# Partition sums by bf16 matmuls, and new orders of work for all five engines, in a decoder layer of attention, cross attention and quantised feed-forward

## The chip, the cores and the metric

The kernel runs on one core of a Trainium2 chip. A time is the device time of one execution in microseconds (us). Before the change, three executions took 2735.64, 2737.21 and 2741.36 us (median 2737.21). The program runs TensorE (PE in the rows, PEld for its weight loads), VectorE (DVE), ScalarE (ACT), GpSimd (POOL) and SyncE (SP), which here issues all DMAs from one queue.

## The reference

The input is 64 independent sequences of 128 tokens by 512 features, with a context of the same shape.

```python
x = layernorm(x + self_attention(x, Wqkv, q_norm_w, k_norm_w, Wo))   # 16 heads, rmsnorm, rope, causal
x = layernorm(x + cross_attention(x, ctx, ctx))                      # 8 heads over the feature axis
x = layernorm(x + quant_dequant(x) @ quant_dequant(W).T)             # fp8 e4m3 in blocks of 128

def cross_attention(q, k, v):          # per batch: q, k, v are 128 x 512; 8 heads of 16 rows
    qk = einsum('bdm,bdn->bmn', qh, kh) * 16 ** -0.5      # 512 x 512 per head
    return einsum('bmn,bcn->bcm', softmax(qk), vh)
```

The kernel keeps fp32-like accuracy by splitting operands in a high and a low fp16 part, and for that scales the input and the context of each batch by a power of two. That power is taken from the sum of squares over the whole 128 x 512 block: ScalarE squares and sums along each partition (`xss`, `css`, 128 x 1 in fp32), TensorE sums over the 128 partitions, and VectorE takes the exponent. Only the exponent of the sum is used.

## The kernel before, in words

One batch is 128 x 512 and is small; the work of a batch is a long chain through all engines. The kernel therefore runs as a pipeline by hand. Each engine has a table (`SP_STEPS`, `POOL_STEPS`, `ACT_STEPS`, `DVE_STEPS`, `PE_STEPS`) with one entry per step of a batch, written `name:part@stage`. In slot t an engine goes through its table once, and does each step for batch t minus stage. A full slot so holds one batch's worth of every step, from up to nine different batches. The tables alone set each engine's order; the engines are held together only by semaphores, and each does its instructions in order, so that one that waits holds up all behind it. The first slots and the last ones are unrolled with the steps of absent batches left out, the middle is a loop over two slots. Where a table is cut into a slot does not matter, only the order of its entries counting stage by stage: with all entries of a table turned round, the instruction stream stays the same.

What the steps are that this text speaks of, with their lines:

- TensorE: `cross_scores` n = 0 to 15 (L1085, into `mx`, two matmuls of 512 columns side by side), read by VectorE's `cross_max` (L811); `cross_scores_T` n = 0 to 15 (L1099, into `st`), read by ScalarE's exponential `probs` (L645); `cross_pv` (L1112); `proj_q`, `proj_k`, `proj_v` and `ffn` in four parts each (L983, three matmuls a part); `proj_o` (L975); `self_scores` (L1017 and L1020), `self_scores_T` (L1030), `self_pv` (L1048, L1051); `context_T` (L968); `x_sum` (L991, L992) and `ctx_sum` (L1073, L1074), the sums over partitions. `mx` and `st` have one buffer each: the next scores wait until the last are read.
- `x_sum` and `ctx_sum` are each two matmuls with one output column: a 128 x 128 matrix of ones times the 128 sums, and the ones times `tiny` (2 to the power -70), which keeps the sum off zero. In fp32 each shows as two passes in the trace (x2). TensorE also does this once for the weights (L956, L957).
- Feed-forward: VectorE and GpSimd quantise in turns (`quant_scale` L920 to L925, `quant_unit` L581, `quant_magic`, `quant_round` L588, L591, L594), ScalarE and GpSimd split the result (`xd_high` L732, `xd_low` L603), the queue transposes it to `xdT` (`turn_xd` L465), and `ffn` reads that.
- Self attention: `rope_terms` (VectorE, L872), `rope_sum` (GpSimd, L547, L548), `part_high` (ScalarE, L675, L676), `part_low` (GpSimd, L552), the transposes `turn_parts` (L414) to `qs` and `ks`; `self_probs` (ScalarE, L695), `mask` (GpSimd, L558), `self_pv`.
- The queue also loads the next context, `ld_cx` (L368). It overwrites the only buffer `cx`, so it waits until `context_T` of the batch before is done.

Of the kernel before, what the change touches and what calls it, by code (L numbers as in the profile page):

```python
# [5 lines left out]
def post_ln_decoder_kernel(nc, x, ctx_in, wqkv, q_norm_w, k_norm_w, wo, wffn, cos_t, sin_t, out):  # L6
    F32, F32R = mybir.dt.float32, mybir.dt.float32r
    BF16, F16, I32 = mybir.dt.bfloat16, mybir.dt.float16, mybir.dt.int32
# [41 lines left out]
    with es:  # L50
        def sb(name, shape, dt=F32):
            return es.enter_context(nc.sbuf_tensor(name, shape, dt))
# [139 lines left out]
        POOL_STEPS = steps("""
            ctx_scale:0@4 layer_rstd:0@3 layer_mean:2@8 context_low:0@4 layer_rstd:2@8 layer_mean:1@7
            mean_square:0@1 layer_rstd:1@7 rope_sum:0@1 mean_square:1@1 part_low:0@1 quant_unit:0@7
            mask:0@2 mask:1@2 rope_sum:1@1 mask:2@2 mask:3@2 cross_scale:0@6 quant_round:0@7
            query_low:0@3 part_low:1@1 oT_low:0@2 quant_round:1@7 quant_round:2@7 xd_low:0@7
            x_scale:0@0 x_low:0@0 cross_scale:1@6 layer_mean:0@2""")
        ACT_STEPS = steps("""
            probs:8@6 layernorm:0@3 square:0@1 layer_devs:1@7 probs:9@6 layernorm:1@7 probs:10@6
            square:1@1 part_high:0@1 self_probs:0@2 probs:11@6 query_high:0@3 value:0@1  # L200
            self_probs:1@2 probs:12@6 x_square:0@0 self_probs:2@2 probs:13@6 self_probs:3@2
            part_high:1@1 probs:14@6 probs:15@6 oT_high:0@2 probs:0@5 context_out:0@4 probs:1@5
            ctx_square:0@3 xd_high:0@7 probs:2@5 x_high:0@0 probs:3@5 probs:4@5 layer_devs:0@2
            probs:5@5 context_high:0@3 probs:6@5 layer_devs:2@7 probs:7@5 layernorm:2@7""")
        DVE_STEPS = steps("""
            self_shift:0@2 cross_max:12@5 rope_terms:0@1 cross_max:13@5 quant_scale:0@7
            cross_max:14@5 cross_max:15@5 rope_terms:1@1 cross_shift:0@5 cross_max:0@4 cross_turn:0@6
            cross_max:1@4 quant_magic:0@7 cross_max:2@4 self_recip:0@2 self_norm:0@2 cross_max:3@4
            x_exp:0@0 cross_max:4@4 cross_turn:1@6 cross_max:5@4 add_self:0@2 cross_max:6@4
            self_max:0@1 ctx_exp:0@3 self_max:1@1 cross_max:7@4 self_max:2@1 cross_max:8@4  # L210
            ctx_inv:0@4 add_ffn:0@7 cross_max:9@4 self_max:3@1 cross_max:10@4 add_cross:0@6
            cross_max:11@4""")
        PE_STEPS = steps("""
            cross_scores_T:10@6 proj_k:2@1 proj_k:3@1 cross_scores:14@5 proj_v:0@1 proj_v:1@1
            self_scores_T:0@2 cross_scores_T:11@6 cross_scores:15@5 proj_v:2@1 proj_v:3@1
            self_scores_T:1@2 cross_scores_T:12@6 cross_scores:0@4 cross_pv:3@6 self_pv:0@2
            self_scores_T:2@2 cross_scores_T:13@6 self_pv:1@2 cross_scores:1@4 self_scores_T:3@2
            cross_pv:4@6 self_pv:2@2 cross_scores:2@4 cross_scores_T:14@6 self_pv:3@2 cross_pv:5@6
            cross_scores_T:15@6 cross_scores:3@4 cross_pv:6@6 context_T:0@4 cross_scores_T:0@5
            x_sum:0@0 cross_pv:7@6 cross_scores:4@4 cross_scores_T:1@5 proj_o:0@2 proj_o:1@2  # L220
            cross_scores:5@4 cross_scores_T:2@5 proj_o:2@2 proj_o:3@2 cross_scores:6@4
            cross_scores_T:3@5 self_scores:0@1 self_scores:1@1 ctx_sum:0@3 cross_pv:0@5
            cross_scores:7@4 cross_scores_T:4@5 self_scores:2@1 ffn:0@7 ffn:1@7 cross_scores_T:5@5
            cross_scores:8@4 ffn:2@7 ffn:3@7 cross_scores_T:6@5 cross_scores:9@4 proj_q:0@0
            self_scores:3@1 cross_scores_T:7@5 cross_scores:10@4 proj_q:1@0 proj_q:2@0
            cross_scores_T:8@5 cross_scores:11@4 proj_q:3@0 proj_k:0@0 proj_k:1@0 cross_scores:12@4
            cross_scores_T:9@5 cross_pv:1@5 cross_pv:2@5 cross_scores:13@4""")
# [924 lines left out]
```

## Time and profile before

| | |
|---|---|
| three timed executions | 2735.64, 2737.21, 2741.36 us |
| the profiled execution | 2741.84 us, its span 2740.1 us |
| TensorE matmuls | 2488.1 us busy, 91% |
| VectorE | 2203.3 us, 80% |
| ScalarE | 2074.7 us, 76% |
| GpSimd | 1670.0 us, 61% |
| mean granted TensorE clock | 0.971 of full speed |

The busy shares are means over the set-up (about 68 us, until the first `x_sum`), the filling of the pipeline, a long steady state, and the run-out in which ever fewer steps are left in a slot. In the steady state the time is the length of a slot times the number of slots, so it is that stretch that has to be read: which engine never waits in it, and for what it waits when it does. The 1.7 us between the span and the time of the same execution lie outside the span.

### The profile page before, as it was taken

The page shows a single profiled execution, that of the slowest core. Times are in us where ns is not written, and L with a number is a line of the kernel's source. Part 1 is how long each engine was busy: PE and PEld are TensorE (multiplying, and loading weights), DVE is VectorE, ACT ScalarE, POOL GpSimd, SP SyncE. Part 2 cuts the span into 40 slices and gives each one's busy share as a digit, 9 for nine tenths or more (in the row PEclk, how much of TensorE's full clock was granted, in tenths as well). Part 3 has the DMA queues.
Part 4 walks back from the last instruction along what each step waited for, and adds up shares of the span by engine and source line. Part 5 has one row for each costly group of instructions (what it writes and reads, how often), then busy time and mean ns, then how long its engine had stood idle before and what let it go on. Part 6 is the DMA issues. An engine that isn't in the chain of part 4 may idle for free.

```text
span 2740.1 us, 67073 instructions
## 1 busy us (share of the span) xinstructions
PE 2488.1 (91%) x19220; PEld 992.2 (36%) x19220; DVE 2203.3 (80%) x3525; ACT 2074.7 (76%) x3097; POOL 1670.0 (61%) x2586
## 2 busy tenths in 40 slices
PE   0679999999999999999999999999999999998874
PEld 0333333343334333333333333433333333433211
DVE  5258888888888888888888888888888888888651
ACT  2237787788888888888888888888888888887553
POOL 1454666666666666666667666666666666765322
PEclk9889999999999999999999999999999999999876
DMA  2345554544454445444554445544544454544211
GB/s 88 66 103 121 119 125 114 129 123 121 119 129 119 128 112 131 121 128 112 127 128 125 115 119 132 123 118 122 128 119 123 117 131 120 130 115 115 71 41 28
DMA packets 610637, 312.01 MB, mean 114 GB/s; under 512 B 469504, under 2 KB 551424, under 8 KB 610560
## 3 DMA queue, kind: packets, MB, share of 16 engines
q1 hardware_dynamic: 610560, 311.06, 45.1%
q8 instruction: 39, 0.64, 0.1%
q14 instruction: 38, 0.31, 0.0%
HBM read 124.80 MB, written 85.46 MB: 77 GB/s over the span
## 4 chain that ended last, share of the span: by engine, by line
PE 65%; SPq 11%; DMA 9%; issue 5%; DVE 5%; POOL 3%; ACT 2%; ACTq 0%; POOLq 0%; DVEq 0%
PE bank L983 25%; PE pv L1112 13%; PE mx L1085 8%; PE st L1099 7%; DMA xdT<-xd 7%; SPq L414 5%; PE bank L1048 2%; PE bank L1030 2%; PE bank L975 2%; PE bank L1051 2%; DVE nm L811 2%; SPq L388 2%; SPq L398 1%; PE bank L968 1%; SPq L379 1%
## 5 line engine op out<-in xcount | busy, mean ns | idle before, releaser
L811 DVE TENSOR_REDUCE nm<-mx 128x2 f32<-128x1024 f32 x1024 | 1248.5, 1219 | 248.7 <-PE mx L1085 241.9
L645 ACT ACTIVATE pp<-st,esc 128x1024 f32<-128x1024 f32 x1024 | 1139.3, 1113 | 341.8 <-PE st L1099 339.1
L1112 PE MATMUL pv<-pp,vT 128*32 128x512 f32 x4096 | 550.3, 622 | 1.2 <-DVE o2t L906 0.9
L983 PE MATMUL bank<-w_h,xsT 128*128 128x512 f16 x1536 | 525.0, 384 | 9.3 <-DMA xsT<-xs 6.3
L1085 PE MATMUL mx<-kp,qp 48*128 48x512 f16 x2048 | 400.7, 388 | 36.9 <-DVE nm L811 34.4
L1099 PE MATMUL st<-qp,kp 50*128 50x512 f16 x2048 | 401.2, 388 | 25.0 <-ACT pp L645 25.0
L983 PE MATMUL bank<-w_l,xsT 128*128 128x512 f16 x768 | 293.0, 381 | 0.0
L983 PE MATMUL bank<-wf_h,xdT 128*128 128x512 f16 x512 | 180.2, 394 | 83.2 <-DMA xdT<-xd 83.1
L983 PEld LDWEIGHTS bank<-w_h,xsT 128*128 128x128 f16 x1536 | 150.1, 98 | 278.2 <-issue 131.1
L534 POOL TENSOR_SCALAR neg_mean<-total 128x1 f32<-128x1 f32 x192 | 36.5, 190 | 329.3 <-DVE yout L938 207.2
L558 POOL TENSOR_SCALAR_AFFINE_SELECT p<-p 128x512 f32<-128x512 f32 x256 | 168.3, 657 | 108.1 <-ACT p L695 103.1
L1085 PEld LDWEIGHTS mx<-kp,qp 48*128 48x128 f16 x2048 | 99.4, 94 | 354.9 <-DVE nm L811 229.4
L872 DVE SCALAR_TENSOR_TENSOR rope<-bank,rms,rope_w 128x1024 f32<-128x1024 f32 x128 | 163.4, 1277 | 37.6 <-POOL rms L514 19.9
L841 DVE TENSOR_REDUCE nm<-bank 128x4 f32<-128x512 f32 x256 | 174.6, 683 | 14.9 <-PE bank L1020 14.9
L1099 PEld LDWEIGHTS st<-qp,kp 50*128 50x128 f16 x2048 | 99.5, 94 | 219.4 <-ACT pp L645 120.9
L695 ACT ACTIVATE p<-bank 128x512 f32<-128x512 f32 x256 | 156.1, 610 | 24.2 <-PE bank L1030 24.1
L511 POOL TENSOR_SCALAR rms<-ssq,xeps 128x1 f32<-128x1 f32 x128 | 33.9, 265 | 192.6 <-ACT junk L669 192.4
L552 POOL TENSOR_TENSOR qkn<-rope,qkn 128x512 f16<-128x512 f32 x128 | 148.0, 1156 | 3.2 <-ACT qkn L676 3.2
L1112 PEld LDWEIGHTS pv<-pp,vT 128*32 128x32 f32 x4096 | 93.6, 110 | 141.4 <-issue 131.8
L711 ACT ACTIVATE x<-x,shift,rstd 128x512 f32<-128x512 f32 x128 | 103.3, 807 | 48.5 <-POOL shift L543 48.5
L975 PE MATMUL bank<-wo_h,oT_h 128*128 128x512 f32 x256 | 116.7, 456 | 6.6 <-POOL oT_l L574 6.6
L539 POOL TENSOR_SCALAR rstd<-devs 128x1 f32<-128x1 f32 x192 | 36.6, 190 | 133.6 <-ACT junkd L706 123.2
(166 smaller groups left out, 4614.1 us busy)
## 6 DMA issues: line engine op xcount, KB each, us to landing
qp<-q_rows SPq DMA_DIRECT2D x256, 96.0 KB, 2.3
kp<-k_rows SPq DMA_DIRECT2D x256, 96.0 KB, 2.2
xb<-x SPq DMA_DIRECT2D x64, 256.0 KB, 2.8
xr<-x SPq DMA_DIRECT2D x64, 256.0 KB, 2.7
x_rows<-x SPq DMA_DIRECT2D x64, 256.0 KB, 2.1
cx<-ctx SPq DMA_DIRECT2D x64, 256.0 KB, 3.0
...
```

Source lines behind the costliest of these rows:

```text
L552: g_.tensor_tensor(qkn[k][:, :, 2 - k, :], rope[:, 0].rearrange("p h a d -> p h (a d)"), qkn[k][:, :, 0, :], ALU.subtract).then_inc(s_part ...
L558: g_.affine_select(out=p1[c % 2][:], in_=p1[c % 2][:], compare_op=ALU.is_ge, fill=0.0, base=0, pattern=[[0, HC], [1, P]], channel_multipli ...
L645: a.activation(pp[:, unit % PB, 2 * l:2 * (l + 1), :], st[:], ACT.Exp, scale=esc[b.i][:])\
L695: a.activation(p1[c % 2][:], at(f"s1t{c}")[:].rearrange("p (h q) -> p h q", h=HC), ACT.Exp, scale=SELF_SCALE).then_inc(bank_free[BANK[f"s1 ...
L811: v.tensor_reduce(cols, mx[:], AX.X, ALU.max, negate=True).then_inc(mx_free, 1)
L841: v.tensor_reduce(nm1[:, HC * c:HC * (c + 1)], at(f"s1m{c}")[:].rearrange("p (h k) -> p h k", h=HC), AX.X, ALU.max, negate=True).then_inc( ...
L872: v.scalar_tensor_tensor(rope[:].rearrange("p t h a d -> p t (h a d)"), at("qk"[k])[:].unsqueeze(1).to_broadcast([P, 2, D]), rms[:, k:k + ...
L975: last = t.matmul(at(name)[:], a[:, rows], w[:, part, cols], start=(part == 0 and i == 0), stop=(part == KC - 1 and i == 2))
L983: last = t.matmul(at(name)[:], lin[:, KC * lo + part, :], w[:, part, cols], start=(part == 0 and i == 0), stop=(part == KC - 1 and i == 2))
L1085: last = t.matmul(mx[:, q, :], qp[b.i][rows, p, c * P:(c + 1) * P], kp[b.i][rows, p, :], start=True, stop=True)
L1099: last = t.matmul(st[:, q, :], kp[b.i][rows, p, i * P:(i + 1) * P], qp[b.i][rows, p, :], start=True, stop=True)
L1112: last = t.matmul(pv[32 * j:32 * j + 2 * XD, :], vT[b.i][:, i, GROUPS * j + g, :], pp[:, unit % PB, j, :], start=(i == 0), stop=(i == KC - 1))
```

## The change

Two edits. First, the ones and `tiny` become bf16, and the moving operand of the sums becomes the upper half of each fp32 word, read in place as bf16 (the lower 16 bits are cut off). `tiny` is two columns wide instead of one. Second, all five tables are written anew. The latest stage goes from 8 to 9, and so there is one slot more (73 for 72); that comes from where the tables are cut, and most steps keep their place relative to the other steps of their engine.

```diff
-        css, cbits, ones = sb("css", [P, 1]), sb("cbits", [P, 1], I32), sb("ones", [P, P])
-        xss, xbits, tiny = sb("xss", [P, 1]), sb("xbits", [P, 1], I32), sb("tiny", [P, 1])
+        css, cbits, ones = sb("css", [P, 1]), sb("cbits", [P, 1], I32), sb("ones", [P, P], BF16)
+        xss, xbits, tiny = sb("xss", [P, 1]), sb("xbits", [P, 1], I32), sb("tiny", [P, 2], BF16)
...
         SP_STEPS = steps("""
-            ld_kp:1@5 st_qpl:0@4 ld_qp:1@5 turn_xd:0@8 turn_x:0@1 ld_x2r:0@7 ld_qp:0@4 ld_x:0@0
...
+            st_sh1:0@3 st_kpl:0@5 st_out:0@9 ld_sh1:0@3 ld_kp:0@5 st_sh2:0@6 ld_sh2:0@6
...
-            t.matmul(mx[:, 0, 0:2], ones[:], wsum[:], start=True, stop=False)
-            t.matmul(mx[:, 0, 0:2], ones[:], tiny[:].to_broadcast([P, 2]), start=False, stop=True).then_inc(u_wtot, 1)
+            t.matmul(mx[:, 0, 0:2], ones[:], wsum[:].bitcast(BF16).rearrange("p (n a) -> p n a", a=2)[:, :, 1], start=True, stop=False)
+            t.matmul(mx[:, 0, 0:2], ones[:], tiny[:], start=False, stop=True).then_inc(u_wtot, 1)
...
-                t.matmul(at("xt")[:, 0:1], ones[:], xss[:], start=True, stop=False)
-                t.matmul(at("xt")[:, 0:1], ones[:], tiny[:], start=False, stop=True).then_inc(bank_full[BANK["xt"]], 1)
+                t.matmul(at("xt")[:, 0:1], ones[:], xss[:].bitcast(BF16)[:, 1:2], start=True, stop=False)
+                t.matmul(at("xt")[:, 0:1], ones[:], tiny[:, 0:1], start=False, stop=True).then_inc(bank_full[BANK["xt"]], 1)
...
-                t.matmul(at("ct")[:, 0:1], ones[:], css[:], start=True, stop=False)
-                t.matmul(at("ct")[:, 0:1], ones[:], tiny[:], start=False, stop=True).then_inc(bank_full[BANK["ct"]], 1)
+                t.matmul(at("ct")[:, 0:1], ones[:], css[:].bitcast(BF16)[:, 1:2], start=True, stop=False)
+                t.matmul(at("ct")[:, 0:1], ones[:], tiny[:, 0:1], start=False, stop=True).then_inc(bank_full[BANK["ct"]], 1)
```

The queue (SP), from the transpose of the query parts to that of the scaled input. `qs` and `ks` are the transposed self-attention parts, `cx` the context, `kp` and `qp` the cross-attention operands, `q_rows` their copy in memory. Before:

```order
L414 DMA_TRANSPOSE qs<-qkn 128x16x128
L368 DMA cx<-ctx 128x512
L414 DMA_TRANSPOSE ks<-qkn 128x16x128
L388 DMA kp<-k_rows 48x2x512 x2
L379 DMA q_rows<-qpl 128x2x512
L380 DMA q_rows<-qpl 128x512
L398 DMA qp<-q_rows 48x2x512 x2
L465 DMA_TRANSPOSE xdT<-xd 128x8x128
L407 DMA_TRANSPOSE xsT<-xs 128x8x128
L458 DMA x<-x_rows 128x512
```

After:

```order
L414 DMA_TRANSPOSE qs<-qkn 128x16x128
L450 DMA x_rows<-x 128x512
L414 DMA_TRANSPOSE ks<-qkn 128x16x128
L388 DMA kp<-k_rows 48x2x512 x2
L368 DMA cx<-ctx 128x512
L465 DMA_TRANSPOSE xdT<-xd 128x8x128
L398 DMA qp<-q_rows 48x2x512 x2
L379 DMA q_rows<-qpl 128x2x512
L380 DMA q_rows<-qpl 128x512
L407 DMA_TRANSPOSE xsT<-xs 128x8x128
L361 DMA xr<-x 128x512
```

The transpose to `xdT` now comes right behind the load of `cx`, ahead of the load of `qp` and the two stores of `q_rows`; the load of `cx` moved behind the transpose to `ks` and the load of `kp`; the store of `x_rows` moved in, and the load of `xr` comes half a slot earlier.

GpSimd (POOL), from the low part of the queries (`qkn`, L552) through the masks (L558) to the low part of the attention output (`oT_l`). Before:

```order
L552 TENSOR_TENSOR qkn<-rope,qkn 128x16x32
L581 TENSOR_TENSOR yq<-x,qri 128x512
L558 AFFINE_SELECT p_0<-p_0 128x512
L558 AFFINE_SELECT p_1<-p_1 128x512
L547 TENSOR_TENSOR rope<-rope 128x16x16
L548 TENSOR_TENSOR rope<-rope 128x16x16
L558 AFFINE_SELECT p_0<-p_0 128x512
L558 AFFINE_SELECT p_1<-p_1 128x512
L609 TENSOR_TENSOR o2n<-o2t,r 128x16x16
L588 TENSOR_TENSOR yq<-yq,yc 128x512
L599 TENSOR_TENSOR qpl<-x,qpl 128x512
L552 TENSOR_TENSOR qkn<-rope,qkn 128x16x32
```

After:

```order
L558 AFFINE_SELECT p_0<-p_0 128x512
L552 TENSOR_TENSOR qkn<-rope,qkn 128x16x32
L558 AFFINE_SELECT p_1<-p_1 128x512
L581 TENSOR_TENSOR yq<-x,qri 128x512
L547 TENSOR_TENSOR rope<-rope 128x16x16
L548 TENSOR_TENSOR rope<-rope 128x16x16
L558 AFFINE_SELECT p_0<-p_0 128x512
L558 AFFINE_SELECT p_1<-p_1 128x512
L588 TENSOR_TENSOR yq<-yq,yc 128x512
L552 TENSOR_TENSOR qkn<-rope,qkn 128x16x32
L591 TENSOR_TENSOR yq<-yq,yc 128x512
L574 TENSOR_TENSOR oT_l<-o,oT_h 128x512
```

The two masks of the first half come before `quant_unit` (L581), the low part of the queries between them. The low part of the cross-attention query (`qpl`) and one scaling (`o2n`) left this stretch; they come behind the low part of `xd` (L603) now.

TensorE, the four `self_pv` (L1048, L1051) and what lies between them. Before:

```order
L1112 MATMUL pv<-pp,vT 32x512 x4
L1048 MATMUL bank<-p_0,va 32x128 x4
L1051 MATMUL bank<-p_0,sums_of 32x128 x4
L1030 MATMUL bank<-qs,ks 128x128 x4
L1099 MATMUL st<-qp,kp 128x512 x2
L1048 MATMUL bank<-p_1,va 32x128 x4
L1051 MATMUL bank<-p_1,sums_of 32x128 x4
L1085 MATMUL mx<-kp,qp 128x512 x2
L1030 MATMUL bank<-qs,ks 128x128 x4
L1112 MATMUL pv<-pp,vT 32x512 x4
L1048 MATMUL bank<-p_0,va 32x128 x4
L1051 MATMUL bank<-p_0,sums_of 32x128 x4
```

After:

```order
L1051 MATMUL bank<-p_0,sums_of 32x128 x4
L1030 MATMUL bank<-qs,ks 128x128 x4
L1048 MATMUL bank<-p_1,va 32x128 x4
L1051 MATMUL bank<-p_1,sums_of 32x128 x4
L1099 MATMUL st<-qp,kp 128x512 x2
L1030 MATMUL bank<-qs,ks 128x128 x4
L1085 MATMUL mx<-kp,qp 128x512 x2
L1112 MATMUL pv<-pp,vT 32x512 x4
L1048 MATMUL bank<-p_0,va 32x128 x4
L1051 MATMUL bank<-p_0,sums_of 32x128 x4
L1048 MATMUL bank<-p_1,va 32x128 x4
L1051 MATMUL bank<-p_1,sums_of 32x128 x4
```

Parts 0 and 1 come sooner behind one another, and parts 2 and 3 (the last four rows) have nothing between them; before, a `cross_scores` and a `cross_scores_T` stood there. On the whole table, `cross_scores_T` moved forward by three to eight places against the other steps of TensorE, `context_T` back by six, and `ffn:0` forward by one.

On ScalarE, `part_high:0` moved from ahead of `self_probs:0` to behind `probs:12` (before: `square:1 part_high:0 self_probs:0 probs:11`; now: `probs:11 square:1 self_probs:0 probs:12 part_high:0`).

## Rows read from the trace of the kernel before

**Rows 1.** Windows of two stretches: length; PE, PEld, DVE, ACT, POOL busy; clock, DMA share
```profile
600.00:2200.00 1600.00, 1557.19 (x12351) 626.91 (x12348) 1389.73 (x2227) 1319.89 (x1978) 1068.91 (x1647) 1.00 0.49 123
2470.00:2741.00 271.00, 190.48 (x1116) 53.60 (x1112) 148.05 (x230) 151.58 (x194) 96.57 (x155) 0.78 0.24 61
```

**Rows 2.** All waits of TensorE's matmuls from 600 to 2200 us (total, times, longest)
```profile
PE bank L983 <- DMA xdT<-xd: 41.4, 41, 1.5
```

**Rows 3.** Timeline of TensorE (start, duration, ...), the first and last full slot's sum
```profile
249.44 0.38 PE L991 MATMUL bank<-xss,ones 128*128 128x1 f32 x2
...
2466.09 0.38 PE L991 MATMUL bank<-xss,ones 128*128 128x1 f32 x2
```

**Rows 4.** Timeline of TensorE, the two sums and what follows each
```profile
1379.59 0.38 PE L991 MATMUL bank<-xss,ones 128*128 128x1 f32 x2
...
1380.12 1.07 PE L1112 MATMUL pv<-pp,vT 128*32 128x512 f32 x8
...
1386.83 0.33 PE L1073 MATMUL bank<-css,ones 128*128 128x1 f32 x2
...
1387.31 1.06 PE L1112 MATMUL pv<-pp,vT 128*32 128x512 f32 x8
```

**Rows 5.** Weight loads of TensorE by line: bf16, and fp32 of one sum
```profile
L1017 PEld LDWEIGHTS bank<-maskb,identb 128*128 128x128 bf16 x256 | 24.9, 97 | 71.1 <-issue 61.3 <-DVE nm L841 1.8 <-DVE cbits L827 0.9
L992 PEld LDWEIGHTS bank<-tiny,ones 128*128 128x128 f32 x128 | 19.9, 196 | 0.0
```

**Rows 6.** Timeline of TensorE, starts from which the prices are read, and the feed-forward product
```profile
1353.57 0.39 PE L983 MATMUL bank<-wf_h,xdT 128*128 128x512 f16 x1
...
1354.97 0.39 PE L1099 MATMUL st<-qp,kp 50*128 50x512 f16 x2
...
1355.51 0.39 PE L983 MATMUL bank<-w_h,xsT 128*128 128x512 f16 x1
...
1370.43 1.06 PE L1112 MATMUL pv<-pp,vT 128*32 128x512 f32 x8
1371.31 0.40 PE L1048 MATMUL bank<-p,va 128*32 128x128 f32 x8
...
1371.87 0.40 PE L1030 MATMUL bank<-qs,ks 98*128 98x128 f16 x4
1372.19 0.39 PE L1099 MATMUL st<-qp,kp 50*128 50x512 f16 x2
...
1375.71 0.42 PE L1048 MATMUL bank<-p,va 128*32 128x128 f32 x8
...
1390.20 0.39 PE L983 MATMUL bank<-wf_h,xdT 128*128 128x512 f16 x1 [0.73 <-DMA xdT<-xd]
```

**Rows 7.** Timeline of the DMA queue's issues (SP)
```profile
1379.51 0.48 SPq L368 DMA_DIRECT2D cx<-ctx  x1
...
1386.90 1.25 SPq L465 DMA_TRANSPOSE xdT<-xd  x1
```

**Rows 8.** DMA issues from 600 to 2200 us, median us to landing
```profile
xdT<-xd SPq DMA_TRANSPOSE x41, 3.2
```

**Rows 9.** Timeline of GpSimd, same slot
```profile
1367.82 1.16 POOL L552 TENSOR_TENSOR qkn<-rope,qkn 128x512 f16<-128x512 f32 x1
1368.94 1.04 POOL L581 TENSOR_TENSOR yq<-x,qri 128x512 f32<-128x512 f32 x1
...
1372.55 0.73 POOL L548 TENSOR_TENSOR rope<-rope 128x256 f32<-128x256 f32 x1
...
1374.85 0.72 POOL L558 TENSOR_SCALAR_AFFINE_SELECT p<-p 128x512 f32<-128x512 f32 x1 [0.85 <-ACT p L695]
...
1384.30 1.17 POOL L603 TENSOR_TENSOR xd<-yq,xd 128x512 f16<-128x512 f32 x1 [0.80 <-ACT xd L732]
```

**Rows 10.** Timeline of ScalarE, same slot
```profile
1367.07 0.62 ACT L676 ACTIVATE qkn<-rope 128x512 f16<-128x512 f32 x1
...
1368.40 1.11 ACT L645 ACTIVATE pp<-st,esc 128x1024 f32<-128x1024 f32 x1
```

More of the change, by code:

```diff
@@ L188, in post_ln_decoder_kernel @@
         SP_STEPS = steps("""
-            ld_kp:1@5 st_qpl:0@4 ld_qp:1@5 turn_xd:0@8 turn_x:0@1 ld_x2r:0@7 ld_qp:0@4 ld_x:0@0
-            st_out:0@8 st_sh1:0@2 st_kpl:0@4 ld_sh1:0@2 ld_kp:0@4 st_sh2:0@5 st_x2:0@3 ld_xr:0@2
-            ld_sh2:0@5 turn_parts:0@1 ld_cx:0@3 turn_parts:1@1""")
+            st_sh1:0@3 st_kpl:0@5 st_out:0@9 ld_sh1:0@3 ld_kp:0@5 st_sh2:0@6 ld_sh2:0@6
+            turn_parts:0@2 st_x2:0@4 turn_parts:1@2 ld_kp:1@5 ld_cx:0@4 turn_xd:0@8 ld_qp:1@5
+            st_qpl:0@4 turn_x:0@1 ld_xr:0@2 ld_x2r:0@7 ld_qp:0@4 ld_x:0@0""")
@@ L192, in post_ln_decoder_kernel @@
         POOL_STEPS = steps("""
[L193 to L197, printed above, removed]
-        ACT_STEPS = steps("""
[L199 to L204, printed above, removed]
@@ L205, in post_ln_decoder_kernel @@
-        DVE_STEPS = steps("""
[L206 to L212, printed above, removed]
@@ L213, in post_ln_decoder_kernel @@
-        PE_STEPS = steps("""
[L214 to L227, printed above, removed]
@@ new lines, in post_ln_decoder_kernel @@
+            layer_rstd:0@3 layer_rstd:2@8 mean_square:0@1 layer_mean:1@7 layer_rstd:1@7 rope_sum:0@1
+            mean_square:1@1 mask:0@2 part_low:0@1 mask:1@2 quant_unit:0@7 rope_sum:1@1 mask:2@2
+            mask:3@2 quant_round:0@7 part_low:1@1 quant_round:1@7 oT_low:0@2 quant_round:2@7
+            x_scale:0@0 xd_low:0@7 query_low:0@3 cross_scale:0@6 cross_scale:1@6 x_low:0@0
+            ctx_scale:0@3 context_low:0@3 layer_mean:0@2 layer_mean:2@7""")
+        ACT_STEPS = steps("""
+            xd_high:0@8 probs:3@6 x_high:0@1 context_out:0@5 probs:4@6 ctx_square:0@4 probs:5@6
+            probs:6@6 context_high:0@4 probs:7@6 layer_devs:0@3 probs:8@6 layer_devs:2@8 probs:9@6
+            square:0@1 layernorm:2@8 layernorm:0@3 layer_devs:1@7 probs:10@6 layernorm:1@7 probs:11@6
+            square:1@1 self_probs:0@2 probs:12@6 part_high:0@1 probs:13@6 self_probs:1@2 value:0@1
+            probs:14@6 self_probs:2@2 x_square:0@0 self_probs:3@2 part_high:1@1 probs:15@6 probs:0@5
+            oT_high:0@2 probs:1@5 query_high:0@3 probs:2@5""")
@@ new lines, in post_ln_decoder_kernel @@
+        DVE_STEPS = steps("""
+            add_ffn:0@8 self_max:3@2 cross_max:10@5 self_shift:0@2 cross_max:11@5 add_cross:0@7
+            cross_max:12@5 rope_terms:0@1 cross_max:13@5 cross_max:14@5 quant_scale:0@7
+            cross_max:15@5 cross_shift:0@5 cross_max:0@4 rope_terms:1@1 cross_max:1@4 cross_turn:0@6
+            quant_magic:0@7 cross_max:2@4 self_recip:0@2 self_norm:0@2 cross_max:3@4 x_exp:0@0
+            ctx_inv:0@4 cross_max:4@4 cross_turn:1@6 cross_max:5@4 cross_max:6@4 self_max:0@1
+            add_self:0@2 self_max:1@1 cross_max:7@4 ctx_exp:0@3 cross_max:8@4 self_max:2@1
+            cross_max:9@4""")
@@ new lines, in post_ln_decoder_kernel @@
+        PE_STEPS = steps("""
+            cross_scores:15@5 proj_v:1@1 proj_v:2@1 cross_scores_T:13@6 cross_scores:0@4
+            self_scores_T:1@2 proj_v:3@1 cross_pv:3@6 cross_scores_T:14@6 cross_scores:1@4
+            self_pv:0@2 self_scores_T:2@2 self_pv:1@2 cross_scores_T:15@6 self_scores_T:3@2
+            cross_scores:2@4 cross_pv:4@6 self_pv:2@2 self_pv:3@2 cross_pv:5@6 cross_scores_T:0@5
+            cross_scores:3@4 x_sum:0@0 cross_pv:6@6 cross_scores_T:1@5 cross_pv:7@6 cross_scores:4@4
+            cross_scores_T:2@5 context_T:0@4 proj_o:0@2 cross_scores:5@4 cross_scores_T:3@5
+            proj_o:1@2 proj_o:2@2 cross_scores:6@4 cross_scores_T:4@5 self_scores:0@1 proj_o:3@2
+            self_scores:1@1 cross_scores_T:5@5 cross_scores:7@4 cross_pv:0@5 ffn:0@7 ctx_sum:0@3
+            cross_scores_T:6@5 cross_scores:8@4 self_scores:2@1 ffn:1@7 cross_scores_T:7@5
+            cross_scores:9@4 ffn:2@7 ffn:3@7 self_scores:3@1 cross_scores_T:8@5 cross_scores:10@4
+            proj_q:0@0 proj_q:1@0 cross_scores_T:9@5 cross_scores:11@4 proj_q:2@0 proj_q:3@0
+            proj_k:0@0 cross_scores:12@4 cross_pv:1@5 cross_pv:2@5 cross_scores_T:10@5
+            cross_scores:13@4 proj_k:1@0 proj_k:2@0 cross_scores_T:11@5 cross_scores:14@4 proj_k:3@0
+            self_scores_T:0@1 proj_v:0@0 cross_scores_T:12@5""")
```

## The prediction

> **What bounds the kernel now.** I read the windows first, then the waits of TensorE, then one slot as a timeline.
>
> From 600 to 2200 us TensorE's matmuls are busy 1557.19 of 1600 us; VectorE 1389.73, ScalarE 1319.89, GpSimd 1068.91, and the granted clock is 1.00, the level of 2.4 GHz [rows 1]. TensorE sits idle 42.8 us, and the one wait that its list shows is for `xdT`, the transposed feed-forward input: 41.4 us in 41 slots, 1.01 us a slot [rows 2]. So TensorE is the bound, with one stall a slot. The length of a slot comes from the first and the last `x_sum` of the full stretch: (2466.09 - 249.44) / 57 = 38.89 us [rows 3]. Of that 1.01 is the stall; 37.9 is work. VectorE has 1389.73 / 1600 x 38.89 = 33.8 us of work a slot, ScalarE 32.1: they have room until a slot is near 34.
>
> A busy PE need not be at its limit, since its intervals overlap. The starts tell: six matmuls of 512 columns and the change to other operands take 1354.97 - 1353.57 = 1.40 us [rows 6], 0.215 us each and about 0.1 for the change, and 512 columns at 2.4 GHz are 0.213 us. The Trainium skill (Perfetto Trace Analysis, Identifying the Most-Contended Engine) warns of just this: matmul busy share is a bad measure, the share of weight loads a better one. By that measure (626.91 of 1600 us, 39%, rows 1) TensorE would have room, another engine would bind, and taking work off TensorE would be worth nothing. Here the trace's spacing speaks against that reading; the result by it is a rival below.
>
> **The sums.** `x_sum` starts at 1379.59 and the next matmul at 1380.12: 0.53 us. `ctx_sum`: 1387.31 - 1386.83 = 0.48 [rows 4]. Together 1.01 us of TensorE a slot, for eight fp32 passes. After the change four bf16 passes are left. No such matmul is in the trace, so two bounds. The dear one: a pass costs what one of the fp32 passes does, (0.53 - 0.1) / 4 = 0.108, so a sum is 0.32 with its change, and 0.38 us a slot is saved. The cheap one: four matmuls of 128 columns with a load each take 1372.19 - 1371.87 = 0.32 with the change [rows 6], 0.055 each, so a sum is 0.21 and 0.59 is saved. I take 0.5, since the bf16 weight load shows 97 ns and the fp32 one 196 [rows 5], which puts the pass nearer to the cheap end. Times 64 batches: **32 us** (24 to 38).
>
> The Trainium skill (TensorE: Matmul & The Clock Gate, LDWEIGHTS) has a rule against part of this: a load costs its columns divided by 1.2, in ns, whatever the width of an element, so about 107 ns for bf16 as for fp32. By it only the number of passes falls: 4 x 0.107 = 0.43 us a slot, 27 us in all. The trace's bf16 row agrees (97), its fp32 row (196) does not, and the sum goes by the rows.
>
> The once-only sum for the weights is worth some 0.5 us and is left out. Reading every second bf16 of a word costs nothing that one column could show. Cutting the lower 16 bits can only move a scale by a factor of two near a boundary, in no instruction's length.
>
> **The stall for xdT.** In the slot shown the low part of `xd` is ready at 1384.30 + 1.17 = 1385.47 [rows 9], but the queue issues the transpose at 1386.90 [rows 7], 1.4 us later: it is behind the load of `cx` (1379.51, held by `context_T`), the transpose to `ks`, the load of `kp`, two stores and the load of `qp`. It lands 3.2 us after its issue [rows 8], and `ffn` starts at 1390.20 having waited 0.73 [rows 6]. In the new order two stores and the `qp` load are behind it, and GpSimd has shed `query_low` and one `cross_scale` ahead of it and taken on `x_scale`. I lay both out against `cross_scores:4`, whose place is the same in both orders (TensorE meets it at 1381.3 in this slot). By the prices below, `ffn:0` is wanted at 1389.2. GpSimd's chain, delayed by the masks as told below, gives `xd_low` done at about 1385.2; the issue at 1385.3, landing at 1388.5. That is 0.7 us before it is wanted, so the stall goes, if nothing holds the queue. The queue's other holder there, `cx`, waits for `context_T`, which TensorE now does at about 1381.8: issue at 1382.6, well before. Gain 1.01 x 57 slots = **58 us**. The `xsT` transpose keeps its time (`x_low` at 1388.9 instead of 1387.6) and is wanted at 1394.7; `ks` is issued sooner.
>
> **New waits.** With the stall gone TensorE runs 37.9 - 0.5 = 37.4 us a slot, and every other chain must fit that. What is tight next is the stretch before the last `self_pv`. `part_high:0` moved behind `probs:12`, and behind it on GpSimd stand `part_low:0`, `mask:1`, `quant_unit`, `rope_sum:1`, `mask:2` and `mask:3`. From the start of `cross_scores_T:12`: its matmuls and change 0.32, `probs:12` 1.11, `part_high:0` 2 x 0.62 [rows 10], `part_low` 1.16, `quant_unit` 1.04, `rope_sum` 2 x 0.73, three masks at 0.65 to 0.72 [rows 9] make 8.3, and five hand-overs at 0.14 (from mask to `self_pv:3`: 1375.71 less 1374.85 + 0.72, rows 6 and 9) make 9.0 us. TensorE's own work from that matmul to `self_pv:3`: four pairs of scores, the last of which is split, at 0.54 (1355.51 - 1354.97) or 0.32 alone, three parts of projection at 0.65 and two changes, two `cross_pv` at 0.88 (1371.31 - 1370.43), three `self_pv` at 0.44 to 0.56 (1371.87 - 1371.31) and three `self_scores_T` at 0.22 to 0.32 [rows 6]: 8.7 us. So `self_pv:3` waits 0.3 us. Before, its mask was done 0.14 us ahead of it, so there was hardly any slack to spend.
>
> In the same way VectorE: sixteen `cross_max` in 37.4 us with one `mx` buffer, `cross_scores` 11 and 14 come within 0.1 us of the reduction before them. And `proj_o:0`, now right behind `context_T`, is 0.4 us behind `oT_low`. I put new waits at 0.35 us a slot, between 0 and 1.0: 57 x 0.35 = **20 us** lost. The row of prices was read at slots where other engines were waited for little, so nothing of it is counted twice.
>
> Moves priced at nothing: `query_high` and `query_low` come some 10 us later, but their store already stood behind both; `layer_mean:0` comes about 5 us later on GpSimd, behind `context_low`, and delays `layer_devs:0` on ScalarE by half a microsecond, ahead of a `cross_scores_T` that TensorE reaches 0.3 us later; `ld_xr` comes half a slot earlier into a free buffer. The cover of all three is TensorE's 37.4 us; if it is gone, they count in the 0 to 1.0. Fill and run-out: the run-out is 274 us from the last `x_sum` [rows 3], at a clock of 0.78 with TensorE idle for a third of it [rows 1], held by the scores' own round trips, which don't change. The extra slot is a matter of where the tables are cut, and empty.
>
> **Sum.** Against the profiled execution's own 2741.8: - 32 - 58 + 20 = - 70, so 2672. The median of the timed runs is 4.6 lower, so **2667 us**: 2.6% less, 37.7 us a slot.
>
> **Rivals.**
> 1. The new waits eat most of it. For it: VectorE at 33.8 and ScalarE at 32.1 of 37.4 us leave little play, and many edges are within 0.5 us. At 0.8 to 1.4 us a slot the gain is 90 - (46 to 80), or 10 to 44: 2693 to 2727. Chance 0.19.
> 2. The transpose is still late, because GpSimd's chain reaches `xd_low` over 0.7 us later than laid out, or the big `cx` load just ahead slows it. Against it: the landing took 3.2 whatever stood ahead. Then only the sums and a part of the stall are gained: 2741.8 - 32 - 20 + 10 = 2700, less 4.6: 2695. Chance 0.12.
> 3. TensorE isn't the bound, so the sums bring nothing, and the stall is only passed on: 2737, no change. The spacing of the matmuls is against it. Chance 0.05.
> 4. Slower: one mechanism, the GpSimd chain before `self_pv:3`. `quant_unit` now stands ahead of `rope_sum:1` and the last two masks, and it waits for VectorE's `quant_scale`, which is behind `cross_max:14`. If VectorE is behind, the masks, `self_pv`, and by them the next slot's `x_sum` all are. It decides from where the chain of 9.0 us passes 8.7 + 1.5, 10.2 us, the 1.5 being what the sums and the stall give. At 10.7 us the slot is 0.5 longer, 57 x 0.5 = 28 us: 2766. Chance 0.07.
>
> The forecast's own case, 2640 to 2692, has 0.57. Its ends: new waits 0 and sums at 0.59 give 2737.2 - 38 - 58 = 2641, and waits of 0.8 give 2692. For the range I go to 2635 below, since gaps of 0.1 to 0.2 us that no row lists could close as well, and to 2727 above, the end of the first rival. Outside lie the third and the fourth and a little below, under 2 in 10. A change below 0.2%, 5.5 us, can't be told from none. Faster by more: 0.57 + 0.19 + 0.12, less a little for the first rival's far end, 0.87; within: 0.05; slower: 0.08.
>
> **What would show it.** After: in a window of the steady state TensorE's idle time for `xdT` near 0, the queue issuing that transpose within 0.3 us of `xd_low`; L991 and L1073 with half the rows and 0.2 to 0.32 us from their start to the next matmul's; the spacing of `x_sum` 37.4 to 38.0; new small waits of L1048 on the masks (L558) under 0.5 us a slot. I am wrong if the spacing is above 38.3, if the `xdT` wait stays over 0.5 us, or if TensorE waits over 1 us a slot for VectorE, ScalarE or GpSimd.

## The result, and the profile after

The changed kernel takes 2635.99 us (median of 2630.81, 2635.99 and 2636.59) against 2737.21: the ratio is 0.9622, with a 95% interval of 0.9597 to 0.9647. That is 101 us less where 70 were forecast; the direction and the kind of gain were right, its size was not. The time lies 4 us below the forecast's own case (2640 to 2692 us) and on the low end of its range, 2635: the median is 1 us inside it, the ratio times the median of before, 2633.7, 1 us outside.

The windows first, with the same columns as [rows 1] (length; PE, PEld, DVE, ACT, POOL busy with counts; granted clock, DMA share, GB/s). Of the kernel after:

```profile
600.00:2200.00 1600.00, 1599.72 (x12753) 616.81 (x12751) 1455.34 (x2328) 1404.55 (x2070) 1118.65 (x1724) 1.00 0.51 128
```

and in three stretches:

```profile
0.00:254.53 254.53, 140.75 (x962) 66.18 (x962) 128.78 (x212) 95.80 (x166) 95.60 (x153) 0.88 0.34 88
254.53:2369.24 2114.71, 2112.84 (x16862) 814.99 (x16861) 1923.51 (x3077) 1855.82 (x2733) 1476.24 (x2273) 1.00 0.52 129
2369.24:2634.90 265.66, 192.10 (x1142) 54.37 (x1140) 150.38 (x238) 156.75 (x200) 102.38 (x161) 0.78 0.25 67
```

TensorE is idle 0.28 us of 1600, where it was 42.8; its list of waits in that stretch is empty, where [rows 2] had 41.4 us for `xdT`. The last three rows are cut at the `x_sum` of the same batches as [rows 3]. The same cuts of the kernel before:

```profile
0.00:249.44 249.44, 140.21 (x995) 70.09 (x995) 129.09 (x214) 96.35 (x167) 97.01 (x155) 0.92 0.36 91
249.44:2466.09 2216.65, 2153.46 (x17090) 866.58 (x17088) 1923.16 (x3077) 1823.35 (x2733) 1472.63 (x2273) 1.00 0.49 123
2466.09:2740.10 274.01, 194.39 (x1140) 55.55 (x1138) 151.06 (x236) 155.04 (x199) 100.37 (x159) 0.79 0.25 64
```

So the fill is 5.1 us longer, the 57 full slots are 101.9 us shorter (38.89 to 37.10 a slot), the run-out 8.3 us shorter: together the 105.2 us by which the spans differ. The gain is in the slot.

Now the sums and the feed-forward product in the timeline of TensorE (start, duration, ...), kernel after, to be held against [rows 4] and [rows 6]:

```profile
1367.31 0.18 PE L991 MATMUL bank<-xss,ones 128*128 128x1 bf16 x1
1367.35 0.16 PE L992 MATMUL bank<-tiny,ones 128*128 128x1 bf16 x1
1367.44 1.06 PE L1112 MATMUL pv<-pp,vT 128*32 128x512 f32 x8
...
1376.63 1.07 PE L1112 MATMUL pv<-pp,vT 128*32 128x512 f32 x8
1377.63 0.39 PE L983 MATMUL bank<-wf_h,xdT 128*128 128x512 f16 x1
...
1378.29 0.17 PE L1073 MATMUL bank<-css,ones 128*128 128x1 bf16 x1
1378.32 0.16 PE L1074 MATMUL bank<-tiny,ones 128*128 128x1 bf16 x1
1378.41 0.39 PE L1099 MATMUL st<-qp,kp 50*128 50x512 f16 x2
```

A sum is one pass instead of two per matmul, and holds TensorE for 0.13 and 0.12 us in all, not 0.53 and 0.48. `ffn` starts with no wait. The queue (SP), same slot, for [rows 7]:

```profile
1371.61 0.36 SPq L368 DMA_DIRECT2D cx<-ctx  x1
1373.61 1.24 SPq L465 DMA_TRANSPOSE xdT<-xd  x1
```

and GpSimd's last operation before it:

```profile
1372.27 1.17 POOL L603 TENSOR_TENSOR xd<-yq,xd 128x512 f16<-128x512 f32 x1
```

The low part of `xd` is ready at 1373.44, the transpose goes out 0.17 us later (1.4 before), and with 3.1 us to landing it is there 0.9 us before 1377.63, where 0.7 was laid out. Counted from `cross_scores:4` (at 1369.77 here), `xd_low` is done after 3.7 us and `ffn:0` starts after 7.9, where 3.9 and 7.9 were laid out. The mechanism of the forecast for the stall is what happened.

### The profile page after: what moved, and what is told of

It is laid out like the page before. It is cut to its first block, busy times and chain, and to the rows that moved or that the text cites. A ratio compares the mean times of both kernels' runs of the same rounds, so it can differ in the third digit from the quotient of the medians.

```text
span 2634.9 us, 66757 instructions
## 1 busy us (share of the span) xinstructions
PE 2445.7 (93%) x18962; PEld 935.5 (36%) x18962; DVE 2202.7 (84%) x3525; ACT 2108.4 (80%) x3097; POOL 1674.2 (64%) x2586
## 4 chain that ended last, share of the span: by engine, by line
PE 89%; DVE 4%; ACT 2%; issue 2%; POOL 2%; DMA 1%; SPq 0%; POOLq 0%; DVEq 0%; ACTq 0%
PE bank L983 26%; PE pv L1112 19%; PE st L1099 12%; PE mx L1085 10%; PE bank L975 8%; PE bank L1048 3%; PE bank L1030 3%; PE bank L1017 3%; PE bank L1020 2%; PE bank L1051 2%; DVE nm L811 1%; PE bank L968 1%; ACT pp L645 1%; DVE rope L872 0%; DMA o<-wffn 0%
## 5 line engine op out<-in xcount | busy, mean ns | idle before, releaser
L1112 PE MATMUL pv<-pp,vT 128*32 128x512 f32 x4096 | 548.2, 621 | 0.2
L983 PE MATMUL bank<-w_h,xsT 128*128 128x512 f16 x1536 | 535.8, 385 | 8.0 <-DMA xsT<-xs 6.3
L983 PE MATMUL bank<-wf_h,xdT 128*128 128x512 f16 x512 | 188.8, 391 | 23.6 <-DMA xdT<-xd 23.6
L558 POOL TENSOR_SCALAR_AFFINE_SELECT p<-p 128x512 f32<-128x512 f32 x256 | 182.6, 723 | 37.7 <-ACT p L695 37.7
L552 POOL TENSOR_TENSOR qkn<-rope,qkn 128x512 f16<-128x512 f32 x128 | 148.1, 1157 | 56.0 <-ACT qkn L676 56.0
L695 ACT ACTIVATE p<-bank 128x512 f32<-128x512 f32 x256 | 152.3, 595 | 14.1 <-PE bank L1030 12.9
L1112 PEld LDWEIGHTS pv<-pp,vT 128*32 128x32 f32 x4096 | 94.6, 110 | 150.4 <-issue 148.0
L669 ACT ACTIVATE junk<-bank 128x512 bf16<-128x512 f32 x128 | 76.0, 594 | 88.9 <-PE bank L983 88.9
L564 POOL TENSOR_SCALAR cxs<-cx,sc 128x512 f32<-128x512 f32 x64 | 44.2, 690 | 157.9 <-DVE sc L831 157.9
L706 ACT ACTIVATE junkd<-x,neg_mean 128x512 bf16<-128x512 f32 x128 | 92.4, 722 | 37.5 <-POOL neg_mean L534 33.8
```

The lines of the kernel that those rows point to most:

```text
L552: g_.tensor_tensor(qkn[k][:, :, 2 - k, :], rope[:, 0].rearrange("p h a d -> p h (a d)"), qkn[k][:, :, 0, :], ALU.subtract).then_inc(s_part ...
L558: g_.affine_select(out=p1[c % 2][:], in_=p1[c % 2][:], compare_op=ALU.is_ge, fill=0.0, base=0, pattern=[[0, HC], [1, P]], channel_multipli ...
L695: a.activation(p1[c % 2][:], at(f"s1t{c}")[:].rearrange("p (h q) -> p h q", h=HC), ACT.Exp, scale=SELF_SCALE).then_inc(bank_free[BANK[f"s1 ...
L983: last = t.matmul(at(name)[:], lin[:, KC * lo + part, :], w[:, part, cols], start=(part == 0 and i == 0), stop=(part == KC - 1 and i == 2))
L1112: last = t.matmul(pv[32 * j:32 * j + 2 * XD, :], vT[b.i][:, i, GROUPS * j + g, :], pp[:, unit % PB, j, :], start=(i == 0), stop=(i == KC - 1))
```

## The experiments

All ratios are to the kernel before, timed beside each run on the same chip; in brackets stands the 95% interval. The kernel before took 2736.23, 2729.51 or 2739.52 us beside them, so where two experiments are compared, the ratio or the length of a slot says more than the time. That length is the mean spacing of `x_sum` from 600 to 2200 us: 38.84 us before the change, 37.12 after it.

**The bf16 sums alone** (all five tables as before; the edit is the first, fourth and later pieces of the diff above).

> The kernel before with the bf16 sums alone, its five orders kept. Theory A (the two edits add up): TensorE's slot loses what the two sums lose in the trace after, 0.77 us (1.01 to 0.24), 64 times: about 49 us less, 2688 us, slot 38.1. Rival B (the sums lie beside the wait for xdT): both sums stand between context_T and ffn:0, and over just that stretch the queue's chain (load of cx, transpose to ks, loads, stores, transpose to xdT) runs beside TensorE. Then TensorE arrives 0.77 us sooner and waits 0.77 us longer: within 5 us of 2737, slot 38.8, the wait for xdT 1.7 us a slot instead of 1.0.

Measured: 2761.29 us, ratio 1.0085 (1.0061 to 1.0109). Neither theory: cheaper sums alone make this kernel slower, by 0.85%. The waits of TensorE's matmuls from 600 to 2200 us (total, times, longest):

```profile
PE bank L983 <- DMA xdT<-xd: 70.4, 41, 2.4
```

Rival B holds for the wait: 1.7 us a slot, where it was 1.0; what TensorE saved it waits. The rest is in the clock. Two neighbouring slots, cut from `x_sum` to `x_sum`:

```profile
1315.80:1354.41 38.61, 37.11 (x299) 14.56 (x297) 33.77 (x55) 32.14 (x49) 25.90 (x41) 1.00 0.50 125
1354.41:1395.06 40.65, 38.63 (x299) 14.81 (x297) 33.55 (x55) 31.90 (x49) 25.86 (x41) 0.96 0.45 116
```

and the timeline of TensorE in the second of them:

```profile
1363.14 0.39 PE L1020 MATMUL bank<-ks,qs 96*128 96x128 f16 x4
1365.52 0.39 PE L983 MATMUL bank<-wf_h,xdT 128*128 128x512 f16 x1 [1.99 <-DMA xdT<-xd]
1365.74 0.38 PE L983 MATMUL bank<-wf_l,xdT 128*128 128x512 f16 x1
1365.95 0.74 PE L983 MATMUL bank<-wf_h,xdT 128*128 128x512 f16 x2
1366.49 0.63 PE L983 MATMUL bank<-wf_l,xdT 128*128 128x512 f16 x1
```

with the window from there on:

```profile
1366.49:1368.00 1.51, 1.51 (x7) 0.28 (x5) 0.00 (x0) 0.00 (x0) 0.00 (x0) 0.50 0.00 0
```

After a wait of 1.99 us the same matmul goes from 0.38 to 0.63 us: the granted clock fell from 1.00 to 0.50, that is from 2.4 to 1.2 GHz, and the slot took 2.0 us more. From 600 to 2200 us it fell so behind 17 of the 41 waits, all of them between 1.64 and 2.37 us long. Waits of that length did not always bring it down (one of 2.18 us did not); none under 1.6 us did. The slots in which it fell took 40.6 us, the others 38.7. In the kernel before the longest wait there was 1.5 us [rows 2], and the clock was 1.00 over that stretch [rows 1]. The Trainium skill (TensorE: Matmul & The Clock Gate, What's actually happening) says that TensorE's clock goes between just these two levels and that lack of activity brings the lower; the rows agree.

**The bf16 sums with other work put in front of the wait.**

```diff
 def ctx_sum(b, _):
+    for _r in range(4):
+        t.matmul(at("ct")[:].rearrange("p (h k) -> p h k", h=HC), identb[:],
+                 maskb[:].unsqueeze(1).to_broadcast([P, HC, P]), start=True, stop=True)
     t.matmul(at("ct")[:, 0:1], ones[:], css[:].bitcast(BF16)[:, 1:2], start=True, stop=False)
```

> The kernel before with the bf16 sums, and in each ctx_sum four more matmuls of 512 columns (identity times mask) whose result is overwritten: 0.86 us more work for TensorE right ahead of its wait for xdT. Theory A (with the bf16 sums alone, TensorE's wait grew to 1.8 to 2.0 us in some slots, its granted clock fell from 2.4 to 1.2 GHz for some us, and those slots took 40.6 us instead of 38.5): the wait shrinks to 0.9 us, the clock stays at 1.00, all slots 38.5 to 38.9, 2730 to 2740 us, 20 to 30 us faster than without the added work. Rival B (the slow slots have another cause, in the queue): they stay, 2755 to 2775 us or more.

Measured: 2728.61 us, ratio 0.9996 (0.9983 to 1.001). From 600 to 2200 us:

```profile
600.00:2200.00 1600.00, 1567.08 (x12375) 618.72 (x12373) 1393.10 (x2231) 1321.45 (x1981) 1069.54 (x1651) 1.00 0.49 124
```

and TensorE's wait in that stretch:

```profile
PE bank L983 <- DMA xdT<-xd: 31.5, 42, 1.3
```

The slot is 38.74 us. The 0.86 us of added matmuls took nothing, since they fill time in which TensorE waited, and gave back the 0.85%: theory A. The extra loss of the sums alone was the clock's.

**The new orders alone** (fp32 sums).

> The five new orders with the old fp32 sums. Theory A: the wait for xdT is gone and TensorE never waits, so the slot is that of after plus what the sums cost more, 37.12 + 0.77 = 37.9: 2636 + 0.77 x 60 = about 2682 us. Rival B: new waits that the cheaper sums hide now would show or vanish with them; a slot under 37.6 or over 38.2 would say that the two edits do not add.

Measured: 2678.36 us, ratio 0.979 (0.9767 to 0.9813), slot 37.82. Theory A. TensorE was busy 1600.00 of 1600 us. Against that kernel the bf16 sums are worth 0.70 us a slot in the kernel after (37.12), so on these orders they are worth their full price: 0.979 to 0.9622 is 46 us. In the new table of TensorE `x_sum` stands ahead of `context_T` and `ctx_sum` right behind `ffn:0`, so neither lies beside the wait any more.

**The new order on the queue alone, in the kernel before**, and **the old order on the queue alone, in the kernel after**.

> The kernel before with fp32 sums, with the new order on the DMA queue alone. Theory A: the wait for xdT came from the queue's order alone; the transpose now goes out when xd_low is ready (1385.5 in the slot shown, 1.4 us sooner), the wait falls from 1.0 to 0.0 to 0.2 us a slot: 2737 - 0.9 x 57 = 2686 us. Rival B: it needs the orders of GpSimd and TensorE as well (xd_low sooner); then over half of the wait is left, 2705 to 2740 us.

> The kernel after with the old order on the DMA queue alone. Theory A: the load of cx waits for context_T, which now comes 3 us later in TensorE's order, and the transposes, loads and stores ahead of turn_xd follow it; xdT lands 3 to 4 us after TensorE wants it, each slot: 2636 + 57 x 3.5 = about 2835 us, slower than before the change. Rival B: the queue's order is worth only the 1.0 us of stall that it took away: 2636 + 58 = 2694 us.

Measured: 3080.5 us, ratio 1.1255 (1.123 to 1.1279), and 2992.56 us, ratio 1.0922 (1.0891 to 1.0953). For the first both theories had the sign wrong. For the second theory A has the sign and the cause, but 2835 us for 2993. In the first, the timeline of ScalarE:

```profile
1291.15 1.12 ACT L645 ACTIVATE pp<-st,esc 128x1024 f32<-128x1024 f32 x1
1296.15 0.63 ACT L652 ACTIVATE junkc<-cx 128x512 bf16<-128x512 f32 x1 [3.89 <-DMA cx<-ctx]
1296.69 0.19 ACT L652 ACTIVATION_READ_ACCUMULATOR junkc<-cx 128x1 f32 x1
1296.78 0.61 ACT L732 ACTIVATE xd<-yq 128x512 f16<-128x512 f32 x1
```

The load of `cx` comes later in the new queue order, and in the old ScalarE order the square of it (L652) stands ahead of `xd_high` (L732) and of the next `probs`. ScalarE waits 3.9 us, TensorE waits for `st` (3.4 us a slot), and the granted clock is 0.92. The transpose that was to go out sooner now waits for the low part of `xd`, 5.0 us a slot; the wait of the queue from 600 to 2200 us:

```profile
SPq L462 <- POOL xd L603: 180.2, 36, 5.3
```

In the second, TensorE waits 4.7 us a slot in all, first for `ks`:

```profile
PE bank L1017 <- DMA ks<-qkn: 91.5, 37, 2.9
PE bank L983 <- DMA xdT<-xd: 42.1, 27, 2.6
PE bank L1030 <- DMA qs<-self_shift: 41.6, 36, 1.4
```

since the `ks` transpose stands behind a load of `cx` that waits for the later `context_T`, 4.5 us a slot on the queue where it was 0.4 in the kernel before:

```profile
SPq L367 <- PE bank L968: 165.9, 37, 4.7
```

Expected was only the wait for `xdT`; that `ks` would come late too, and cost more, was overlooked.

**One entry moved on the queue**, with fp32 and then with bf16 sums.

```diff
-            ld_kp:1@5 st_qpl:0@4 ld_qp:1@5 turn_xd:0@8 turn_x:0@1 ld_x2r:0@7 ld_qp:0@4 ld_x:0@0
+            ld_kp:1@5 turn_xd:0@8 st_qpl:0@4 ld_qp:1@5 turn_x:0@1 ld_x2r:0@7 ld_qp:0@4 ld_x:0@0
```

> The kernel before (fp32 sums, old orders) with one entry moved: the transpose to xdT goes out ahead of the two stores of q_rows and the load of qp. Theory A (the stall of 1.2 us a slot is the 1.4 us that these three held the queue after xd_low was ready): the stall falls to 0 to 0.2 us, slot 37.8, 2737 - 60 = 2677 us, as with all five new orders. Rival B (another wait takes its place at once, since the xsT transpose and the stores come 1.4 us later): over 2700 us.

> The same one move with the bf16 sums. Theory A: the sums give back 0.7 us of TensorE a slot but half of it lies over the queue's chain from context_T, which becomes the bound: slot 37.3 to 37.6, 2645 to 2665 us, the clock at 1.00. Rival B (the five tables are needed): TensorE again waits over 1 us a slot for xdT, 2690 us or more.

Measured: 2708.0 us, ratio 0.9885 (0.9861 to 0.9908), and 2702.5 us, ratio 0.9869 (0.9846 to 0.9893). In the first this is rival B. In the second the time is that of rival B, but not its wait. The wait for `xdT` is gone, and another is there. TensorE's waits in the second of the two kernels:

```profile
PE mx L1085 <- DMA qp<-q_rows: 35.0, 42, 1.3
PE bank L983 <- DMA xdT<-xd: 1.5, 9, 0.2
```

`cross_scores:8` now waits for the `qp` half that the transpose overtook. The slot is 38.2 us in both kernels, so a chain through the queue sets it, and the sums bring nothing in the slot (the 5.5 us between the two times lie mainly in the run-out, 273.6 and 269.0 us in the two traces). The queue's own waits in the second kernel name what it stands for there:

```profile
SPq L462 <- POOL xd L603: 36.5, 42, 1.5
SPq L367 <- PE bank L968: 15.6, 41, 0.5
```

At the transpose to `xdT` the queue now waits 0.9 us a slot for the low part of `xd` (1.0 with fp32 sums), and the two stores and the load of `qp` wait behind it; in the kernel before they went out in that time. At the load of `cx` it waits only 0.4 us for `context_T`. So what holds `qp` is first GpSimd's chain to `xd_low`. How that chain closes back to TensorE no run tested. The new tables have the same queue wait (61.7 us in 43 slots), but TensorE waits for nothing behind it.

**The price of a pass.** Eight more matmuls of the ones by `tiny` in each sum:

```diff
+                for _r in range(8):
+                    t.matmul(at("xt")[:, 0:1], ones[:], tiny[:, 0:1], start=False, stop=False)
                 t.matmul(at("xt")[:, 0:1], ones[:], tiny[:, 0:1], start=False, stop=True).then_inc(bank_full[BANK["xt"]], 1)
```

> The kernel after with eight more bf16 matmuls of one column (ones times tiny) in each of the two sums, 16 a slot, added into the same column. Theory A (a one-column bf16 pass holds TensorE for about 0.03 to 0.04 us, as the starts after show): 16 x 0.035 = 0.56 us a slot, about 36 us more, 2672 us. Rival B (0.055 us, the price of a 128-column matmul with its load): 0.88 us a slot, 2692 us. Rival C (0.107, the price of an fp32 pass): 1.7 us a slot, 2745 us.

Measured: 2657.51 us, ratio 0.973 (0.971 to 0.9751), slot 37.50 for 37.12: 0.38 / 16 = 0.024 us a pass, under all three theories' prices. The Trainium skill (TensorE: Matmul & The Clock Gate, Back-to-back issue gap) gives a floor of about 25 ns for matmuls of 1 to 64 columns; the run agrees.

**`part_high:0` back at its old place** on ScalarE.

```diff
-... square:1@1 self_probs:0@2 probs:12@6 part_high:0@1 ...
+... square:1@1 part_high:0@1 self_probs:0@2 probs:12@6 ...
```

> The kernel after with part_high:0 put back ahead of self_probs:0 on ScalarE. Theory A (the wait of 0.18 us of the last self_pv for its mask comes from this chain, and the place was chosen well otherwise): self_probs:0 and probs:12 come 1.24 us later, cross_scores_T:13 then waits about 1 us for probs:12: slot 38.1, 2636 + 57 = 2693 us. Rival B (it only takes away the wait): slot 36.95, 2626 us.

Measured: 2686.17 us, ratio 0.9836 (0.9816 to 0.9855), slot 37.86. Theory A, with 0.74 us for the 1.0 expected. The wait that it made, for the exponential of the cross-attention scores, is named:

```profile
PE st L1093 <- ACT pp L639: 24.4, 42, 0.6
```

(lines are six lower in this file). An exchange of 1.2 us of work on an engine that is busy 88% of the time costs 2.1% (0.9836 for 0.9622). The wait of the last `self_pv` did not go with it: from L1051 to L1048 (lines of the kernel after) it is 0.43 us there for 0.41, so the old place would not have saved it.

**Without the mask matmuls** (the causal mask is left out ahead of the row maximum of self attention, so that the maximum, which only shifts the exponent, is taken over masked entries too).

```diff
-                t.matmul(at(name)[:].rearrange("p (h k) -> p h k", h=HC), identb[:],
-                         maskb[:].unsqueeze(1).to_broadcast([P, HC, P]), start=True, stop=False)
...
-                                    ks[0:SROWS, HC * c + j, :], start=False, stop=(j == HC - 1))
+                                    ks[0:SROWS, HC * c + j, :], start=True, stop=True)
```

> The kernel after without the four matmuls a slot that add the causal mask ahead of the row maximum of self attention (L1017); the maximum is then taken over masked entries too, which only changes the shift that is subtracted before the exponential. Theory A (TensorE alone bounds the slot): 4 x 0.22 = 0.9 us a slot less, 36.2 us, 2636 - 0.9 x 60 = 2582 us. Rival B (VectorE, with 33.8 us of work in a slot of 37.1, or ScalarE's chain takes over at once): under half of it, 2610 to 2640 us.

> The kernel after without the four mask matmuls, beside after itself. Theory A: the slot was 36.91 us against 37.12, so 0.21 x 60 = 12 us less than after in the same call, ratio to after 0.995. Rival B: no difference that can be told.

> The kernel after, unchanged, beside the others of this call: 0.962 of before, whatever the theory.

Measured: 2624.17 us, ratio 0.9609 (0.9591 to 0.9628); repeated beside the kernel after, 2626.86 us, ratio 0.959 (0.9567 to 0.9613), where the kernel after has 2632.82 us, ratio 0.9611 (0.9588 to 0.9635). The slot is 36.91 us: 0.21 less for 0.90 us of work taken away. Rival B of the first expectation. All of TensorE's listed waits:

```profile
PE mx L1083 <- DVE nm L811: 9.0, 44, 0.2
```

The larger part is in starts that come late without being listed (waits under 0.15 us are not): the eleven places where `cross_scores` follows `cross_scores_T` took 2.64 us a slot after the change and 3.17 here. Three of the eleven are later, by 0.12, 0.19 and 0.22 us, and each of them starts 0.06 us after VectorE's reduction has freed `mx`; only the last is in the list. One of them stood 0.15 us late in the kernel after already. At 37.1 us TensorE is the bound by a hair; at 36.9 it shares it. This is the fastest version of all. Beside the kernel after it takes 6 us less where 12 were expected: all four of its times (2625.28 to 2628.27) are below all four of the other (2630.11 to 2634.09), though the intervals of the two ratios overlap.

## Why the prediction came out short

The form of the sum held: one stall that goes, the sums, new waits, and fill and run-out nearly unchanged (-3 us net). What failed is the size of all three terms, each 0.16 to 0.20 us a slot too low in gain: the stall was priced by its idle row alone, the price of a sum had a lower bound (0.21 us) that was none, and the new waits were put at more than twice what came. All numbers are starts to starts of TensorE's matmuls, averaged over about 40 slots.

1. **The stall.** Forecast 1.01 us a slot, the idle time of [rows 2]. From the start of the `self_scores` (L1020) before `ffn:0` to `ffn:0` it was 1.40 us, and after, from such a start to a product of the same kind, 0.225: 1.17. The idle time of a row begins when the last matmul's modelled end is past, and that end is 0.16 us after the moment at which the next could have started (a matmul of 128 columns lasts 0.22 at a spacing of 0.055). A stall costs its idle row plus that overlap. With one stall a slot that is 57 x 0.16 = 9 us.
2. **The sums.** Forecast 0.5 us a slot, bounds 0.38 and 0.59; measured 0.70 by the slot (37.82 to 37.12), 0.71 by the starts. The failed step is the lower bound of the price: "four matmuls of 128 columns with a load each", 0.055 us each. That is no bound for one column. A pass of one column holds TensorE 0.024 us when it repeats the same ones (above), and a sum 0.13 with the change of operands. I bounded from the nearest row and took it as an end. 57 x 0.20 = 11 us more.
3. **New waits.** Forecast 0.35 us a slot between 0 and 1.0. The orders alone gain 1.02 (38.84 to 37.82) where the stall was worth 1.17, so they cost 0.15. The one that I worked out was right in place and nearly in size: the last `self_pv` pair, timelines of TensorE and of GpSimd, kernel after:

```profile
1401.83 0.40 PE L1048 MATMUL bank<-p,va 128*32 128x128 f32 x8
1402.04 0.40 PE L1051 MATMUL bank<-p,sums_of 128*32 128x128 f32 x8
1402.45 0.42 PE L1048 MATMUL bank<-p,va 128*32 128x128 f32 x8
```

```profile
1400.80 1.60 POOL L558 TENSOR_SCALAR_AFFINE_SELECT p<-p 128x512 f32<-128x512 f32 x2
```

From L1051 to L1048 it is 0.41 us here where 0.22 is the unhindered spacing (L1051 to L1112): a wait of 0.19, forecast 0.3. The last mask ends at 1402.40, 0.05 us before that start, and so in every slot: it is the mask that is waited for. From `cross_scores_T:12` (1393.50) to `self_pv:3` it is 8.95 us, where 9.0 were laid out, and 8.76 without the wait, where 8.7 were. That the chain came out so close is in part luck: the 0.14 us taken for a hand-over was slack (a start that waits for the mask comes 0.05 us after it), and GpSimd waited 0.42 us for `self_probs:1` (L695) ahead of `mask:1`, which the forecast left out. What I added for VectorE and `proj_o` (another 0.05) did not come: the one `cross_scores` that starts right at the end of VectorE's reduction was 0.20 us late before the change and is 0.15 late now. And `context_T` followed by `proj_o` costs 0.41 us, both being fp32, where `context_T` followed by `cross_scores_T` cost 0.59, which I had priced as equal. What makes up the rest of the 0.15 was not traced. 57 x 0.20 = 11 us more.

Together 0.56 us a slot, 32 us. The full slots gained 102 us where 1.16 x 57 = 66 were forecast for them. Of the 36 us between, 32 are the three terms; the other 4 lie in the slots before 600 us, where the gain was larger. From profiled execution to profiled execution it is 105 us for 70. The medians show only 101, because the profiled execution of the kernel before was 4.6 us above its median and that of the kernel after 0.6: the 4.6 us that the forecast took off were chance, and they hide 4 us of its error.

The signs that the forecast named say the same. The transpose goes out within 0.3 us of `xd_low`, the wait for `xdT` is gone and the new waits are small, as told; but the spacing of `x_sum` is 37.1 us, below its 37.4 to 38.0, and a sum holds TensorE for 0.13 us, below its 0.2 to 0.32. Both miss on the side of the gain.

Adding the terms was right only for this change. The sums alone were worth less than nothing, and one queue move half of the stall: the forecast did not say that the 32 us depend on the stall being gone, though in the old tables `x_sum` and `ctx_sum` both stand between `context_T` and `ffn:0`, beside the queue's chain.

Of the rivals: the first (new waits of 0.8 us or more) did not come, nor the second (the transpose went out 0.17 us after `xd_low`). The third, that TensorE is not the bound, is false for the sums on the new orders, which were worth their full price, and true for them on the old ones; and it lies only 0.2 us of slot away, as the run without the mask matmuls shows. The fourth did not come: its chain passes TensorE's own work by 0.19 us, not by 1.5, and no run tested where its point of decision lies. That a chain of ScalarE, moved by 1.2 us, costs 0.74 us a slot, the run with `part_high:0` at its old place shows.
